# Adj tiles stored in memory as four column pieces

## The chip, the cores and the metric
The kernel runs on one core of a Trainium2 chip. The metric is the time of one execution on the device in microseconds, lower is better; of several runs the median counts.

## The reference
N = 4096 rows, D = 512. `adj` is a sparse 0/1 matrix whose entries get rarer with growing row and column number.
```
q = x @ Wq.T + bq ;  k = key @ Wk.T + bk ;  v = value @ Wv.T + bv
s = (q @ k.T) / sqrt(4096) * adj
s = where(|s| < 1e-5, -1e9, s)
out = layernorm(x + softmax(s) @ v @ Wm.T + bm)
```

## The kernel before
Rows are split into T = 32 row tiles of 128 rows (row r*32 + t is in tile t). In each row tile only few of the 4096 columns have an entry in adj. The kernel finds these columns, gathers the rows of key, of the projected values and of the transposed adj that belong to them (CH = 3 chunks of 128 slots per tile), and does dense attention on 384 slots.

*Reading adj.* The host has laid adj out as `adj_tiles[t]`, 128 x 4096 floats, 16 KB in a row for each partition, 2 MB a tile. SP loads tile t into one of two buffers (`load_adj`, L326 to L329), as soon as the DVE has freed it. The DVE folds each tile with an OR of its two halves (L898), which frees the buffer, and three steps of max and one reduction (L901 to L909) into flags per group of columns. After 8 tiles PE transposes the flags (`lists`), and the DVE picks the slots by six rounds of max and replace (`take_8`, L931, L933) and writes indices.

*First stage.* SP's queue holds, in this order: wv in pieces, the constants, adj tiles 0 to 3, wq and wk, adj tiles 4 to 19, the x tiles 0 to 3, eight copies from `key` into the left half of a `table` in memory (L353, 512 rows of 2 KB each), adj tile 20, a block of xT, adj tile 21. ACT's queue holds wmT and eight blocks of valueT (L715, rows of 8 KB), and between them the value rows that PE and ACT have made, as eight writes into the right half of `table` (L729, 2 KB pieces). PE makes the value rows (L487) and the first q block (L496). GpSimd gathers keys, adj columns and, once the value rows have landed, values for row tiles 0 and 1; for row tile 2 and later it gathers whole table rows (4 KB, L392) and waits for all copies of key before the first (L444).

*Second stage.* PE goes through 32 row tiles: scores, values of the tile before, transposes of the next keys (L578) and adj columns (L593), a q unit (L496), transposes of the weights (L612). In iteration i the DVE takes the score product (`soften`, L1030), the weights (L1045), the sum with x (L1061) and then one more adj tile (`reduce_tile`) of the tiles 20 to 31. SP issues one x tile (waiting for L1061 of the iteration) and behind it the next adj tile, so a tile is loaded during one iteration and used in the next. From row tile 16 on the slots come from these later tiles.

Of the kernel before, what the change touches and what calls it, by code (L numbers as in the profile page):

```python
# [12 lines left out]
P = 128  # L13
N = 4096
D = 512
DC = D // P
T = N // P
# [19 lines left out]
INV_SCALE = 1.0 / float(N) ** 0.5  # L37
MASKED = -1e9
TINY = 1e-5

C_ID = 0
C_DESC = C_ID + P
# [16 lines left out]
def build(nc, adj_tiles, adj_cols, key, valueT, x, xT, wq, wk, wv, wmT, bm, consts, table, out):  # L59
    with ExitStack() as ctx:  # L60
# [3 lines left out]
        def sem(name):  # L64
            return ctx.enter_context(nc.semaphore(name))
# [26 lines left out]
        adj_buf = [big[:, i * 4096:(i + 1) * 4096] for i in range(2)]  # L92
# [66 lines left out]
        adj_in = [sem(f"adj_in{i}") for i in range(2)]  # L159
# [119 lines left out]
        def one_tile(ap, t):  # L279
            return ap[bass.ds(t, 1)].rearrange("a p d -> p (a d)")  # L280

        def wait_apart(eng, s, value):
            eng.wait_ge(s, value)
            eng.sem_inc(passed, 1)

        def trees_of(i):

            t = FIRST + i - (i > LIST_AT[2])
            return [t] if i != LIST_AT[2] and t < T else []
# [13 lines left out]
        def finish_of(i):  # L303

            return sqrt_of(i) if i >= T - 1 else sqrt_of(i - 1)
# [4 lines left out]
        @contextmanager  # L310
        def overflow(eng):
            eng.wait_ge(rounds_ready, 1)
            n = eng.value_load(rounds_i[0:1, 0:1], min_val=0, max_val=MAXR)
            with eng.If(n > 0):
                eng.wait_ge(again, 1)
                yield n
# [3 lines left out]
        @block.sync  # L320
        def _(sp):
            def load_xT(nb):
                sp.wait_ge(q_ps, DC * (nb - 1))
                sp.dma_start(col_buf[nb % 2], xT[nb]).then_inc(cols_in[nb % 2], 16)

            def load_adj(t):  # L326
                if t >= 2:
                    sp.wait_ge(adj_used, t - 1)
                sp.dma_start(adj_buf[t % 2], adj_tiles[t]).then_inc(adj_in[t % 2], 16)  # L329

            def load_x(t):
                if t >= XB:
                    sp.wait_ge(y_sb, t - XB + 1)
                sp.dma_start(x_buf[:, t % XB, :], x_tiles[t]).then_inc(x_in[t % XB], 16)

            def store(t):
                sp.wait_ge(fin_sb, t + 1)
                sp.dma_start(out_tiles[t], y_buf[:, t % YB, :]).then_inc(stored[t % YB], 16)

            for e in range(DC):  # L340
                sp.dma_start(v_left[:, e, :], wv[e * P:(e + 1) * P, :]).then_inc(weights2_in[e], 16)
            sp.dma_start(cst[:, :], consts).then_inc(cst_in, 16)
            sp.dma_start(bm_row, bm).then_inc(bm_in, 16)
            for t in range(4):
                load_adj(t)
            sp.dma_start(w_left, wq.rearrange("(e p) d -> p e d", p=P)).then_inc(weights_in, 16)
            sp.dma_start(w_right, wk.rearrange("(e p) d -> p e d", p=P)).then_inc(weights_in, 16)
            for t in range(4, FIRST):
                load_adj(t)
            for t in range(XB):  # L350
                load_x(t)
            for nb in range(NB):
                sp.dma_start(table[nb * 512:(nb + 1) * 512, 0:D], key[nb * 512:(nb + 1) * 512, :]).then_inc(table_in, 16)  # L353
            for t in trees_of(0):
                load_adj(t)
            for i in range(T + 1):
                for t in finish_of(i - 1):
                    store(t)
                if i % 4 == 0 and i // 4 + 2 < NB:
                    load_xT(i // 4 + 2)  # L360
                if i >= 1 and i + XB - 1 < T:
                    load_x(i + XB - 1)
                for t in trees_of(i + 1):
                    load_adj(t)
            for t in finish_of(T):
                store(t)
            for i in range(YB):
                sp.wait_ge(stored[i], 16 * (T // YB))
            sp.sem_inc(again, 1)

            with overflow(sp) as n:
                with sp.Fori(0, n) as r:
                    with sp.Fori(0, NB) as nb:
                        wait_apart(sp, g_q_sb, (r * NB + nb) * DC + 1)
                        sp.dma_start(g_xT, xT[bass.ds(nb, 1)].rearrange("a p d n -> p (a d) n")).then_inc(g_xT_in, 16)
                sp.wait_ge(g_p_all, 2)
                with sp.Fori(0, T) as t:
                    sp.dma_start(g_x, one_tile(x_tiles, t)).then_inc(g_x_in, 16)
                    wait_apart(sp, g_fin, t + 1)
                    sp.dma_start(one_tile(out_tiles, t), g_y).then_inc(g_stored, 16)  # L380
                    wait_apart(sp, g_stored, t * 16 + 16)
# [495 lines left out]
        def _(dve):  # L877
# [144 lines left out]
            def soften(t):  # L1022
# [9 lines left out]
                dve.wait_ge(abs_sb, t + 1)  # L1032
                nc.vector.tensor_scalar(size[:, :], size[:, :], TINY, MASKED, ALU.is_lt, ALU.mult).then_inc(tiny_sb, 1)
                dve.wait_ge(tiny_sb, t + 1)
# [71 lines left out]
            with overflow(dve) as n:  # L1106
# [7 lines left out]
                with dve.Fori(0, n) as r:  # L1114
# [21 lines left out]
                    with dve.Fori(0, NB) as nb:  # L1136
                        block_no = r * NB + nb
                        for j in range(4):
# [6 lines left out]
                            wait_apart(dve, g_soft, it * 4 + 1)  # L1145
                            nc.vector.tensor_scalar(size[:, :], score[:, 0:SLOTS], TINY, MASKED, ALU.is_lt, ALU.mult
                                                    ).then_inc(g_soft, 1)
                            wait_apart(dve, g_soft, it * 4 + 2)
                            nc.vector.scalar_tensor_tensor(size[:, :], score[:, 0:SLOTS], -TINY, size[:, :],
                                                           ALU.is_gt, ALU.mult).then_inc(g_soft, 1)  # L1150
# [60 lines left out]
def layout(adj, key, value, x, Wq, Wk, Wv, Wm, bq, bk, bv, bm):  # L1211

    import numpy as np

    a = adj.reshape(P, T, K4, P, G8)
    const = np.zeros((P, C_ALL), np.float32)
    p = np.arange(P)
    const[:, C_ID:C_ID + P] = np.eye(P)
    const[:, C_DESC:C_DESC + GK] = GK - np.arange(GK)

    const[:, C_GRP:C_GRP + P] = (p % G8)[:, None] == (p // SPC)[None, :]
    const[:, C_SEL:C_SEL + BT] = (p // G8)[:, None] == np.arange(BT)[None, :]

    const[:, C_BK] = N + p // SPC
    const[:, C_BA:C_BA + T] = (T * (N + p // SPC))[:, None] + np.arange(T)[None, :]
    const[:, C_THR:C_THR + MAXR - 1] = [GS * q for q in range(1, MAXR)]
    const[:, C_NEG] = MASKED
    const[:, C_EPS] = 1e-5
    const[:, C_BV] = 2 * const[:, C_BK] + 1
    const[:, C_TWO] = 2.0 * (p % G8 == G8 - 1)  # L1230
    const[:, C_GRP2:C_GRP2 + P] = const[:, C_GRP:C_GRP + P]
    const[:, C_GRP2 + P - 2:C_GRP2 + P] = 0.0
    for i, b in enumerate((bq, bk, bv)):
        const[:, C_B + i * DC:C_B + (i + 1) * DC] = b.reshape(DC, P).T
    return {
        "adj_tiles": np.ascontiguousarray(a.transpose(1, 3, 0, 2, 4)).reshape(T, P, N),
        "adj_cols": np.concatenate([adj.reshape(P, T, N).transpose(2, 1, 0).reshape(N * T, P),
                                    np.zeros((G8 * T, P), adj.dtype)]),
        "key": key,
        "valueT": np.ascontiguousarray(value.reshape(NB, 512, DC, P).transpose(0, 3, 2, 1)),  # L1240
        "x": x,
        "xT": np.ascontiguousarray(x.reshape(P, NB, T // NB, DC, P).transpose(1, 4, 3, 2, 0)).reshape(NB, P, DC, 512),
        "wq": Wq, "wk": Wk, "wv": Wv, "wmT": np.ascontiguousarray(Wm.T),
        "bm": bm.reshape(1, D),
        "consts": const,
    }
# [19 lines left out]
```

## Time and profile before

| | |
|---|---|
| median of 3 runs | 562.37 us (561.5 to 562.74) |
| the profiled execution | 560.05 us, of it 558.2 us from first to last instruction (span) |
| busy, share of the span | PE 92%, DVE 60%, POOL 42%, ACT 41% |
| mean DMA rate | 288 GB/s, 160.81 MB moved |
| DMA queue q1 (SP) | 20,690 packets, 102.21 MB |
| DMA queue q10 (ACT) | 6,240 packets, 19.92 MB |
| DMA queue q0 (GpSimd) | 16,992 packets, 38.26 MB |
| granted TensorE clock, mean | 0.973 |

The mean shares hide stages: PE is busy nearly throughout, but with different things ahead of it. The tables by stretches of time and the chain of waits have to be read before one can say what a transfer is worth.

### The profile page before, as it was taken

The numbers are of one execution on the slowest core, as the hardware profiler recorded it, in microseconds if no ns is written. First come the engines' busy times: TensorE is split into PE (matmuls) and PEld (weight loads), VectorE is DVE, ScalarE is ACT, GpSimd is POOL, SyncE is SP. The second block draws the span as 40 slices with busy tenths as digits, with TensorE's granted clock in tenths as the row PEclk, the third lists the DMA queues.
The fourth block names the chain that finished last, engine by engine and source line by source line (L and its number), as shares of the span: only waits on it lengthen the run. The fifth ranks groups of instructions, "written<-read, shape, count | busy, mean of one in ns | idle before, by whom it ended". The sixth has DMA issues, their size and how long they took to land.

```text
span 558.2 us, 5679 instructions
## 1 busy us (share of the span) xinstructions
PE 510.8 (92%) x1678; PEld 267.3 (48%) x1678; DVE 337.4 (60%) x756; ACT 229.7 (41%) x463; POOL 232.0 (42%) x205
## 2 busy tenths in 40 slices
PE   6999999999389974999999989999999999999983
PEld 3444444444134443556555545555555555555651
DVE  1574678976961047678688888765645543453552
ACT  0233123333123222334552554464373464465473
POOL 3000020008600366466675565655664565466400
PEclk9999999999879996999999999999999999999996
DMA  9999999999999999595899899656547455346422
GB/s 350 423 406 426 426 422 387 384 397 418 408 395 356 340 418 389 175 360 206 320 383 408 318 292 354 217 162 212 164 150 242 105 182 187 99 144 227 114 76 79
DMA packets 43957, 160.81 MB, mean 288 GB/s; under 512 B 9874, under 2 KB 9874, under 8 KB 37778
## 3 DMA queue, kind: packets, MB, share of 16 engines
q1 hardware_dynamic: 20690, 102.21, 47.0%
q0 software_dynamic: 16992, 38.26, 22.3%
q10 hardware_dynamic: 6240, 19.92, 9.0%
q8 instruction: 15, 0.25, 0.2%
q14 instruction: 20, 0.16, 0.1%
HBM read 161.98 MB, written 25.17 MB: 335 GB/s over the span
## 4 chain that ended last, share of the span: by engine, by line
PE 43%; DMA 22%; DVE 19%; SPq 8%; ACT 4%; issue 3%; POOL 0%; ACTq 0%; DVEq 0%; POOLq 0%
DMA big<-adj_tiles 16%; PE bank L496 13%; PE bank L602 11%; PE bank L622 10%; SPq L353 7%; DVE big L898 7%; PE bank L578 5%; DMA table<-key 4%; DMA kv<-table,index 2%; PE bank L612 1%; DVE big L933 1%; DVE slots L931 1%; PE bank L593 1%; DVE big L901 1%; DVE score L1035 1%
## 5 line engine op out<-in xcount | busy, mean ns | idle before, releaser
L392 POOL DMA_INDIRECT kv<-table,index x90 | 100.1, 1112 | 111.5 <-PE bank L622 89.2
L487 PE MATMUL bank<-kv,big 128*128 128x512 f32 x256 | 113.6, 604 | 10.6 <-DMA big<-valueT 10.6
L496 PE MATMUL bank<-big,M 128*128 128x512 f32 x256 | 120.0, 596 | 0.0
L421 POOL DMA_INDIRECT adj_g<-adj_cols,index x96 | 107.8, 1123 | 29.3 <-issue 29.3
L898 DVE TENSOR_TENSOR big<-big 128x2048 bf16<-128x2048 f32 x32 | 73.2, 2288 | 41.3 <-DMA big<-adj_tiles 41.3
L602 PE MATMUL bank<-keyT,qT 128*128 128x384 f32 x256 | 88.9, 490 | 6.2 <-issue 4.9
L622 PE MATMUL bank<-kv,probT 128*128 128x512 f32 x192 | 89.7, 604 | 0.9 <-ACT probT L809 0.6
L487 PEld LDWEIGHTS bank<-kv,big 128*128 128x128 f32 x256 | 49.1, 193 | 72.6 <-issue 61.0
L602 PEld LDWEIGHTS bank<-keyT,qT 128*128 128x128 f32 x256 | 47.6, 190 | 46.7 <-issue 19.1
L496 PEld LDWEIGHTS bank<-big,M 128*128 128x128 f32 x256 | 44.6, 192 | 34.2 <-issue 34.2
L1030 DVE SCALAR_TENSOR_TENSOR score<-bank,c_cols,adjT 128x384 f32<-128x384 f32 x32 | 19.8, 618 | 67.8 <-PE bank L602 66.4
L578 PEld LDWEIGHTS bank<-cst,kv 128*128 128x128 f32 x384 | 44.9, 144 | 26.4 <-issue 15.5
L578 PE MATMUL bank<-cst,kv 128*128 128x128 f32 x384 | 48.6, 278 | 9.1 <-DMA kv<-table,index 8.3
L622 PEld LDWEIGHTS bank<-kv,probT 128*128 128x128 f32 x192 | 36.7, 193 | 41.0 <-issue 32.6
L783 ACT ACTIVATE keyT<-bank 128x512 f32<-128x512 f32 x96 | 50.2, 592 | 5.1 <-PE bank L578 5.1
L795 ACT ACTIVATE size<-score 128x384 f32<-128x384 f32 x32 | 16.6, 518 | 79.2 <-DVE score L1030 79.2
L772 ACT ACTIVATE qT<-bank,u_col 128x512 f32<-128x512 f32 x32 | 22.0, 687 | 41.5 <-PE bank L496 41.5
L802 ACT ACTIVATE score<-score,new_max 128x384 f32<-128x384 f32 x32 | 19.7, 616 | 40.3 <-DVE new_max L1038 40.3
L428 POOL MEMSET kv<- 128x4096 f32 x1 | 3.5, 3511 | 67.9 <-PE bank L546 67.9
L1045 DVE TENSOR_SCALAR score<-score 128x382 f32<-128x382 f32 x32 | 13.7, 428 | 23.7 <-ACT score L802 23.7
L724 ACT ACTIVATE qT<-bank 128x512 f32<-128x512 f32 x16 | 9.6, 597 | 43.3 <-PE bank L487 43.3
L402 POOL DMA_INDIRECT kv<-key,index x6 | 7.3, 1222 | 48.0 <-DVE index L951 46.5
(99 smaller groups left out, 522.4 us busy)
## 6 DMA issues: line engine op xcount, KB each, us to landing
big<-adj_tiles SPq DMA_DIRECT2D x32, 2048.0 KB, 11.3
big<-valueT ACTq DMA_DIRECT2D x8, 1024.0 KB, 13.4
x_buf<-x SPq DMA_DIRECT2D x32, 256.0 KB, 4.5
table<-key SPq DMA_DIRECT2D x8, 1024.0 KB, 22.8
out<-y_buf SPq DMA_DIRECT2D x32, 256.0 KB, 3.7
big<-xT SPq DMA_DIRECT2D x6, 1024.0 KB, 12.0
table<-qT ACTq DMA_DIRECT2D x4, 1024.0 KB, 20.9
table<-y_buf ACTq DMA_DIRECT2D x4, 1024.0 KB, 28.5
```

What stands on the lines that cost most here:

```text
L353: sp.dma_start(table[nb * 512:(nb + 1) * 512, 0:D], key[nb * 512:(nb + 1) * 512, :]).then_inc(table_in, 16)
L392: pool.indirect_dma_start(kv[:, b, c, :], None, table, bass.IndirectOffsetOnAxis(index[:, t, c:c + 1], 0), bounds_check=N - 1, oob_is_err= ...
L421: pool.indirect_dma_start(adj_g[:, b, c, :], None, adj_cols, bass.IndirectOffsetOnAxis(index[:, t, CH + c:CH + c + 1], 0),).then_inc(adj_g ...
L487: mm = nc.tensor.matmul(bank[4 + t % 2][:, :], col_buf[nb % 2][:, d, k * P:(k + 1) * P], G[:, d, :], start=(d == 0), stop=(d == DC - 1))
L496: mm = nc.tensor.matmul(ps[:, :], M[:, d, a * P:(a + 1) * P], col_buf[nb % 2][:, d, :], start=(d == 0), stop=(d == DC - 1))
L578: mm = nc.tensor.transpose(key_bank[c][:, a * P:(a + 1) * P], kv[:, t % KV, c, a * P:(a + 1) * P], ident)
L602: mm = nc.tensor.matmul(bank[3][:, 0:SLOTS], qT[:, t // 4 % QB, a, t % 4 * P:(t % 4 + 1) * P], keyT[:, a, :], start=(a == 0), stop=(a == D ...
L622: mm = nc.tensor.matmul(bank[5][:, :], probT[:, c * P:(c + 1) * P], kv[:, t % KV, c, D:2 * D], start=(c == 0), stop=(c == CH - 1))
L772: nc.scalar.activation(qT[:, nb % QB, a, :], ps[:, :], ACT.Identity, bias=u_col[:, a:a + 1]).then_inc(q_sb, 1)
L783: nc.scalar.activation(keyT[:, :, c * P:(c + 1) * P], key_bank[c][:, :].rearrange("p (a k) -> p a k", a=DC), ACT.Copy).then_inc(keyT_sb, 1)
L898: nc.vector.tensor_tensor(t1, adj_buf[t % 2][:, 0:2048], adj_buf[t % 2][:, 2048:4096], ALU.logical_or).then_inc(adj_used, 1)
L1030: nc.vector.scalar_tensor_tensor(s, bank[3][:, 0:SLOTS], c_cols[:, t:t + 1], adjT[:, :], ALU.add, ALU.mult).then_inc(prod_sb, 1)
```

## The change
The host lays each adj tile out as four pieces of 1024 columns, each 128 x 1024 floats. A partition's 16 KB are then four runs of 4 KB, 512 KB apart. The load names the buffer as (partition, piece, column) and the source in the same order, so the buffer receives the same bytes at the same places. Nothing else changes: the count of loads, their order and their semaphores stay.
```diff
+PIECES = 4
...
-                sp.dma_start(adj_buf[t % 2], adj_tiles[t]).then_inc(adj_in[t % 2], 16)
+                sp.dma_start(adj_buf[t % 2].rearrange("p (j n) -> p j n", j=PIECES), adj_tiles[t].rearrange("j p n -> p j n")
+                             ).then_inc(adj_in[t % 2], 16)
...
-        "adj_tiles": np.ascontiguousarray(a.transpose(1, 3, 0, 2, 4)).reshape(T, P, N),
+        "adj_tiles": np.ascontiguousarray(
+            a.transpose(1, 3, 0, 2, 4).reshape(T, P, PIECES, N // PIECES).transpose(0, 2, 1, 3)),
```

## Rows read from the trace of the kernel before

**Rows 1.** Windows table: window, length, busy us (instructions) per engine, granted clock, DMA share, GB/s
```profile
0.00:141.00 141.00, 136.67 (x323) 60.29 (x324) 91.54 (x148) 39.34 (x92) 23.26 (x16) 1.00 1.00 404
141.00:201.00 60.00, 46.50 (x133) 22.36 (x132) 25.81 (x59) 15.94 (x34) 15.60 (x16) 0.91 1.03 377
201.00:217.00 16.00, 7.38 (x20) 3.27 (x19) 9.03 (x19) 2.91 (x7) 12.55 (x11) 0.81 0.99 396
217.00:268.00 51.00, 50.18 (x190) 29.34 (x189) 38.09 (x79) 20.09 (x41) 28.96 (x24) 0.96 0.73 267
268.00:336.00 68.00, 62.40 (x234) 34.72 (x233) 54.24 (x122) 34.95 (x67) 43.05 (x37) 1.00 0.95 349
336.00:558.00 222.00, 207.69 (x784) 117.30 (x784) 118.69 (x333) 116.51 (x224) 108.57 (x105) 0.98 0.53 169
```

**Rows 2.** View of one line, L329: its issues, ns min/median/max, first to last start
```profile
L329 SPq DMA_DIRECT2D big<-adj_tiles x32: 327/334/3622, 3.6 to 337.6; - x32
```

**Rows 3.** Chain of waits, 140 to 217 us: start us, us, what
```profile
140.41 0.33 SPq L329
...
180.26 20.32 DMA table<-key
...
204.01 12.64 DMA kv<-table,index
```

**Rows 4.** Timeline of GpSimd: start us, us, instruction, idle before it and releaser
```profile
201.40 1.00 POOL L392 DMA_INDIRECT kv<-table,index  x1 [3.37 <-DMA table<-key]
```

**Rows 5.** Timeline of PE, same columns
```profile
155.14 16.22 PE L487 MATMUL bank<-kv,big 128*128 128x512 f32 x32 [10.60 <-DMA big<-valueT]
...
216.69 2.82 PE L578 MATMUL bank<-cst,kv 128*128 128x128 f32 x12 [8.32 <-DMA kv<-table,index]
...
232.79 0.49 PE L612 MATMUL bank<-cst,score 128*128 128x128 f32 x3
```

**Rows 6.** DMA view, 52 to 58 us; by queue: packets, MB, share of 16 engines
```profile
q1 hardware_dynamic: 144, 2.11, 82.2%
q10 hardware_dynamic: 223, 0.46, 19.5%
```

**Rows 7.** DMA view, 36 to 39.5 us (wq and wk, rows of 2 KB)
```profile
DMA packets 625, 1.42 MB, mean 406 GB/s; under 512 B 29, under 2 KB 29, under 8 KB 611
```

**Rows 8.** DMA view, 206 to 211 us
```profile
q1 hardware_dynamic: 103, 1.32, 62.5%
q0 software_dynamic: 277, 0.69, 36.8%
```

**Rows 9.** DMA view, 160 to 171 us, queue of SP (copies of key, beside q10)
```profile
q1 hardware_dynamic: 1157, 2.30, 60.4%
```

**Rows 10.** DMA view, 186 to 190 us, queue of SP (copies of key, nearly alone)
```profile
q1 hardware_dynamic: 666, 1.32, 102.4%
```

**Rows 11.** Timeline of the DVE: start us, us, instruction, idle before it and releaser
```profile
206.06 2.29 DVE L898 TENSOR_TENSOR big<-big 128x2048 bf16<-128x2048 f32 x1 [5.56 <-DMA big<-adj_tiles]
...
216.81 2.27 DVE L898 TENSOR_TENSOR big<-big 128x2048 bf16<-128x2048 f32 x1
...
227.06 0.62 DVE L1030 SCALAR_TENSOR_TENSOR score<-bank,c_cols,adjT 128x384 f32<-128x384 f32 x1 [5.18 <-PE bank L602]
...
230.20 0.42 DVE L1045 TENSOR_SCALAR score<-score 128x382 f32<-128x382 f32 x1 [0.78 <-ACT score L802]
```

**Rows 12.** Timeline of SP, one issue of an adj tile
```profile
288.29 0.43 SPq L329 DMA_DIRECT2D big<-adj_tiles  x1
```

**Rows 13.** View of L329, its issues from 264 to 326 us, time to landing
```profile
DMA to landing us min/median/max: 9.6/10.7/11.3
```

**Rows 14.** Chain of waits, start of the OR of one tile
```profile
300.79 2.29 DVE big L898
```

**Rows 15.** DMA view, 60 to 141 us, queue of SP
```profile
q1 hardware_dynamic: 1642, 24.02, 73.4%
```

**Rows 16.** Page, DMA issues: what, count, KB each, median us to landing
```profile
big<-valueT ACTq DMA_DIRECT2D x8, 1024.0 KB, 13.4
```

## The prediction

> **What bounds the kernel now.** I read the windows table first, because this kernel has stages with different limits [rows 1]. Its column "DMA share" is the busy share of the 16 DMA engines. Up to 217 us it stands at 0.99 to 1.03: the transfers never rest. From 217 to 268 it is 0.73 while PE is busy for 50.2 of 51 us, from 268 to 336 DVE shares the chain with PE, and after 336 us PE is busy for 208 of 222 us with DMA at 0.53. The last adj tile is issued at 337.6 us [rows 2]. So the change can only act at three places: the saturated stretch, its end, and the stretch from 268 to 336.
>
> The chain of waits says what ends the saturated stretch. The DVE works through adj tiles 0 to 19, mostly waiting for the next tile. When it frees a buffer at 140.41 us SP issues tile 19, then four x loads and eight copies of key into the table; the last copy is issued at 180.26 and lands 20.32 us later, at T = 200.6 [rows 3]. GpSimd has waited 3.37 us for exactly that [rows 4], issues the three gathers of row tile 2, the last at 204.01, and PE, which idled for 8.3 us, starts on them at 216.69 [rows 3, 5]. From there on PE leads. So two numbers matter: when T comes, and how long the gather takes after T (16.05 us).
>
> **The change, part by part.** The same 2 MB per tile arrive, at the same places of the buffer, and no DVE, PE or ACT instruction changes. Each partition's 16 KB now come as four runs of 4 KB that lie 512 KB apart. A DMA engine moves 8 partitions of a tile, so it gets 32 packets of 4 KB where it had 8 of 16 KB. Three things follow, and a fourth at the end.
>
> *1. More packets on saturated engines.* Between 52 and 58 us both sizes run side by side [rows 6]. q1: 2.11 MB are 129 packets of 16 KB; 82.2% of 16 x 6 us are 78.9 us, 612 ns each. q10: 0.46 MB are about 223 packets of 2 KB; 18.7 us, 84 ns each. With time = fixed + bytes x rate this gives 0.0368 ns per byte and 8.6 ns fixed per packet. Then 24 more packets per tile and engine cost 0.21 us, 4.1 us for the 20 tiles before T. A second reading is by rates: 2.57 MB in 6 us are 428 GB/s in that window, 406 where 2 KB rows of the weights run almost alone [rows 7]. A tile of 2.10 MB is 4.90 or 5.17 us; 0.27 us over 56 more packets is 4.8 ns each, so 24 of them are 0.12 us, 2.3 us for 20 tiles. Ends: 2.3 us and, if 4 KB were as dear as 2 KB, 5.4 us. I take 3.2 us, between the two readings. Nothing hides it: the share is 1.00 before 141 us and 1.03 after.
>
> The Trainium skill (DMA: Bandwidth & Descriptors, "iDMA fabric — 4 AXI ports for 8 engines, asymmetric across TPBs") has 408.7 GB/s for a stream of loads with 4 KiB rows; at that rate a tile would take 5.13 us, 0.23 us more than at 428 GB/s, and 20 tiles 4.6 us, 1.4 us more than I take. No row here has such loads on SP's queue.
>
> *2. A different split between the queues.* Where two queues have work, the packets alternate. From 206 to 211 us q1 moves 1.32 MB in xT and adj packets, about 100, and q0 moves 0.69 MB, about 170 packets of at most 4 KB; q1 takes 62.5% of the time and q0 36.8% [rows 8]. One for one, with a few engines already out of q1 work, gives that. With 4 KB packets adj gets a smaller share beside ACT's queue (valueT, value rows of the table) and those land sooner. PE's one stall of the first stage, 10.6 us for valueT at 155.14 us [rows 5], should nearly go. It is off the chain: PE waits for the gather anyhow, so this only makes its later idle longer. T itself needs all of that traffic done, in whatever order, and the engines were full before, so the order alone does not move T. One side effect does. The key copies then run more by themselves. From 160 to 171 us beside q10 a 2 KB packet of theirs took 60.4% of 176 us over 1123 packets, 95 ns [rows 9]; alone, from 186 to 190 us, 102.4% of 64 us over 645, 102 ns [rows 10]. There are 256 per engine: 0 if nothing shifts, 1.8 us if all did. I take 1.2 us.
>
> *3. The gather after T.* On the engine that reaches T last, q1 still holds tile 20 (8 packets), an xT block (8 of about 306 ns, half of 612) and tile 21 (8): 12.3 us. The gather of row tile 2 has 24 packets per engine; by size one is 8.6 + 4096 x 0.0368 = 159 ns. I let its first packets come at T + 2.8: it is issued at T + 0.8, and with 2 us from there the count meets the trace, as follows. Alternating from there, q1's remaining 19.4 packets (9.5 us) pair with 19.4 gather packets (3.1 us), and 4.6 gather packets follow (0.7 us): T + 16.1. The trace has T + 16.05. With 4 KB packets q1 has 17.6 of tile 20's 32 done by T + 2.8; then 24 pairs, 14.4 with adj (0.318 us), 8 with xT (0.465 us), 1.6 with adj: 8.8 us. The gather ends at T + 11.6, 4.4 us sooner.
>
> Some of it is lost on the DVE, which now gets its tiles later. Tile 20 landed at T + 5.4 (DVE starts at 206.06 after 5.56 us of waiting [rows 11]); alternating it lands at about T + 7.4. Tile 21 was there before the DVE asked for it at 216.81; now, paired with the gathers of row tile 3, it lands at about T + 20. The DVE can then start the score product of row tile 2 at T + 25.3 (5.1 us after that OR, as 227.06 - 5.18 - 216.81 [rows 11]), where PE would offer it at T + 22.0 (227.06 less 4.4). These 3.3 us meet 2.0 us of slack: the weights are ready at about 230.8 and PE transposes them at 232.79 [rows 5, 11]. So 1.3 us are given back and 3.1 us kept. Ends: 0 (the DVE eats it all, or packets do not alternate) and 4.4.
>
> The Trainium skill (same page, "Queues, rings and completion order") says that a DMA engine drains a whole packet of typically 9 to 17 descriptors of one ring before it switches. Taken literally the split would go by groups of about the same bytes for q0 and this part would give 0 instead of 3.1 us. The counts of [rows 8] do not tell groups of 8 from single ones; the two readings part only after the change.
>
> *4. The stretch from 268 to 336 us.* SP issues a tile once per iteration. The one issued at 288.29 landed 11.3 us later, at 299.6, and the DVE began on it at 300.79 [rows 12, 13, 14]: 1.2 us of slack. The tiles issued from 264 to 326 us took 9.6 to 11.3 us. A tile gets 0.12 to 0.21 us longer by packets and somewhat more from the adj_g gathers that run beside it. SP's own instruction is a DMA issue of 0.43 us and may grow; the copies of key show that the queue takes 512 rows per DMA. Below the slack this costs 0; at 1 us too late per tile it would be 6 us. I take 0.3 us.
>
> **Sum.** +3.2 + 1.2 - 3.1 + 0.3 = +1.6 us. The profiled execution had 558.2 us of span in 560.05 us; the median of the runs is 562.37. So 559.8 in span and 564.0 as a time.
>
> **Rivals.**
> *Stalls of the 16 KB packets go (faster).* From 60 to 141 us q1's 1466 data packets took 73.4% of 1296 us, 649 ns each instead of 612 [rows 15]. Something slows reads for a while. If it is how 16 engines walk through 16 KB rows in step, a layout with other distances ends it: 37 ns x 8 packets x 11.5 tiles is 3.4 us, which turns 564.0 into 560.6. It decides from 1.6 us of relief on. For it: the slow packets were in a stretch with adj nearly alone. Against: the same share could be paid by any layout, and the new one could also add such stalls (the same 3.4 us upward, 567.4). Chance 0.24.
> *No alternation gain (slower).* The gather still lands at T + 16, because an engine serves the queues in larger groups or the DVE's late tiles hold everything: 564.0 + 3.1 = 567.1. Chance 0.17.
> *Late tiles (slower).* From 268 to 336 us tiles land over 1.2 us later than now, and the DVE waits in each of some six iterations. At 2 us late beyond the slack over three to six tiles: +6 to +12, about 571. Decides from 12.5 us issue to landing. Chance 0.08.
> *Nothing (same).* Costs and gain cancel or the packets are priced by bytes: 562.4. Chance 0.13.
> *Forecast*, 562.9 to 565.5: chance 0.38.
>
> **Numbers.** A measurement of this kernel tells changes of about 0.2%, 1.1 us. The forecast is just above that bound, so of its 0.38 some 0.11 are within it. Faster by over 0.2%: 0.24 plus a little of the others, 0.26. Within: 0.13 + 0.11 + 0.02 = 0.26. Slower: 0.48. The range holds the stall relief on one side and the missing gather gain with 4 KB as dear as 2 KB on the other: 559.5 to 568.5; late tiles and a larger relief stay outside.
>
> **What would show it.** q1 has some 12,300 packets more. Landing of valueT and of the value rows well below before (valueT 13.4 us, median [rows 16]), PE's stall at 155 us gone. T at 203 to 206 us. From T to PE's restart 11 to 14 us instead of 16. DVE waiting for tile 20 and tile 21. Tiles after 268 us landing in 10 to 12.5 us with no DVE wait. The prediction is wrong if T moves by less than 2 or more than 6 us, or if PE restarts as long after T as now.

## The result, and the profile after

The changed kernel takes 571.59 us (median of 4 runs, 569.89 to 571.98), the kernel before 561.93 us (4 runs in the same comparison): ratio 1.0175, 95% interval 1.0133 to 1.0217. I had forecast 564.0 us within 559.5 to 568.5. It is slower, as forecast, but by 9.7 us instead of 1.6, and outside the range. The profiled execution took 571.98 us with 570.1 us of span. It lies 11.9 us above the profiled one of the kernel before, while the medians lie 9.7 us apart, so what the traces show below is a little larger than the typical difference.

The queues in the changed kernel, from its page (queue: packets, MB, share of 16 engines), show that the packets changed as expected: 12,288 more on q1, the same bytes.
```profile
q1 hardware_dynamic: 32978, 102.21, 47.6%
q10 hardware_dynamic: 6240, 19.92, 8.9%
```
The windows table of the changed kernel (columns as in [rows 1]):
```profile
60.00:90.00 30.00, 30.00 (x73) 13.27 (x71) 19.94 (x22) 7.49 (x19) 3.51 (x1) 1.00 0.95 356
90.00:115.00 25.00, 18.07 (x45) 7.77 (x44) 16.39 (x34) 7.35 (x18) 0.00 (x0) 0.92 1.02 403
115.00:125.00 10.00, 4.73 (x11) 2.95 (x12) 9.66 (x19) 0.00 (x0) 0.00 (x0) 0.53 0.31 105
125.00:165.00 40.00, 40.00 (x97) 17.63 (x97) 19.14 (x30) 13.61 (x33) 21.06 (x18) 1.00 1.01 400
```
and two of the same windows in the kernel before:
```profile
60.00:90.00 30.00, 30.00 (x73) 13.35 (x72) 20.30 (x25) 8.00 (x20) 3.51 (x1) 1.00 1.02 415
115.00:125.00 10.00, 10.00 (x25) 4.42 (x24) 6.26 (x16) 3.73 (x9) 1.07 (x1) 1.00 1.01 398
```
There is a hole: from 115 to 125 us the DMA engines are busy for 0.31 of the time where they were full, 6.9 us of transfer time lost, and PE is busy for half of the window. Already from 60 to 90 us the engines move 356 GB/s instead of 415. No window of [rows 1] before 217 us has such a hole.

The waits that make the hole, from PE's timeline of the changed kernel (start us, us, instruction, idle before it and releaser):
```profile
120.27 1.42 PE L518 MATMUL bank<-cst,big 64*128 64x8 f32 x6 [12.20 <-DVE big L941]
...
188.35 5.84 PE L562 MATMUL bank<-kv,keyT 128*128 128x512 f32 x8 [16.49 <-DVE keyT L1019]
...
228.93 1.63 PE L580 MATMUL bank<-cst,kv 128*128 128x128 f32 x12 [2.90 <-DMA kv<-table,index]
```
and from the DVE's, first of the kernel before, then of the changed one:
```profile
90.10 2.29 DVE L898 TENSOR_TENSOR big<-big 128x2048 bf16<-128x2048 f32 x1 [0.46 <-DMA big<-adj_tiles]
```
```profile
103.92 2.29 DVE L900 TENSOR_TENSOR big<-big 128x2048 bf16<-128x2048 f32 x1 [2.92 <-DMA big<-adj_tiles]
```
This is the OR of tile 11, the last before the DVE makes the first list. It comes 13.8 us later. PE reaches unit 17, behind which it spreads that list's slots (L516 before, L518 now), at 108 us as ever, but the list is ready only at 120 us. In the kernel before the list was ready at 106.7 us (end of L939), 1.9 us before PE came to L516 at 108.64. The stall at 155.14 us for valueT [rows 5] is gone, as predicted; these two came instead. While PE waits it makes no value rows, so ACT's queue has nothing to load or store. The DVE works on the list and frees no adj buffer, so SP's queue has nothing to load either. Both queues run dry together. In the kernel before the DVE made the same list, SP's queue ran dry just the same, and ACT's queue filled the engines alone (DMA view, 105 to 110 us, then the changed kernel, 115 to 125 us):
```profile
q10 hardware_dynamic: 660, 2.03, 100.4%
q1 hardware_dynamic: 1, 0.00, 0.0%
```
```profile
q1 hardware_dynamic: 257, 0.99, 29.0%
q10 hardware_dynamic: 42, 0.07, 1.8%
```

The key copies then land late. GpSimd's first gather from the table, changed kernel (answers to [rows 4]), and the chain around it (answers to [rows 3]):
```profile
215.00 1.00 POOL L394 DMA_INDIRECT kv<-table,index  x1 [8.60 <-DMA table<-key]
```
```profile
195.10 19.09 DMA table<-key
217.60 11.28 DMA kv<-table,index
```
T is 214.2 instead of 200.6, 13.6 us later. The gather ends 14.7 us after it instead of 16.05. PE restarts at 228.93 instead of 216.69, 12.2 us later, and the span is 11.9 us longer. The whole loss is made before T. The other stall, 16.49 us for L1019, is not on the way to T: the key copies on SP's queue do not wait for it, and in e9 below it is longer (22.32 us) while T comes 7.1 us sooner.

### The profile page after: what moved, and what is told of

The parts are those of the page before. It is cut to its first block, busy times and chain, and to the rows that moved or that the text cites. A ratio compares the mean times of both kernels' runs of the same rounds, so it can differ in the third digit from the quotient of the medians.

```text
span 570.1 us, 5679 instructions
## 1 busy us (share of the span) xinstructions
PE 511.6 (90%) x1678; PEld 267.2 (47%) x1678; DVE 336.4 (59%) x756; ACT 229.5 (40%) x463; POOL 231.0 (41%) x205
## 4 chain that ended last, share of the span: by engine, by line
PE 45%; DMA 26%; DVE 16%; SPq 5%; issue 4%; ACT 3%; POOL 0%; ACTq 0%; DVEq 0%; POOLq 0%
DMA big<-adj_tiles 21%; PE bank L498 14%; PE bank L604 11%; PE bank L624 11%; DVE big L900 6%; PE bank L580 5%; SPq L355 5%; DMA table<-key 3%; DMA kv<-table,index 2%; PE bank L614 1%; PE bank L595 1%; DVE big L935 1%; DVE slots L933 1%; DVE big L903 1%; DVE score L1037 1%
## 5 line engine op out<-in xcount | busy, mean ns | idle before, releaser
L394 POOL DMA_INDIRECT kv<-table,index x90 | 96.5, 1072 | 114.9 <-PE bank L624 86.9
L423 POOL DMA_INDIRECT adj_g<-adj_cols,index x96 | 111.6, 1162 | 29.3 <-issue 29.3
L580 PE MATMUL bank<-cst,kv 128*128 128x128 f32 x384 | 47.4, 273 | 3.7 <-DMA kv<-table,index 2.9
L774 ACT ACTIVATE qT<-bank,u_col 128x512 f32<-128x512 f32 x32 | 22.0, 687 | 41.4 <-PE bank L498 31.4
## 6 DMA issues: line engine op xcount, KB each, us to landing
table<-qT ACTq DMA_DIRECT2D x4, 1024.0 KB, 15.6
table<-y_buf ACTq DMA_DIRECT2D x4, 1024.0 KB, 16.8
```

Source lines behind the costliest of these rows:

```text
L394: pool.indirect_dma_start(kv[:, b, c, :], None, table, bass.IndirectOffsetOnAxis(index[:, t, c:c + 1], 0), bounds_check=N - 1, oob_is_err= ...
L423: pool.indirect_dma_start(adj_g[:, b, c, :], None, adj_cols, bass.IndirectOffsetOnAxis(index[:, t, CH + c:CH + c + 1], 0),).then_inc(adj_g ...
L580: mm = nc.tensor.transpose(key_bank[c][:, a * P:(a + 1) * P], kv[:, t % KV, c, a * P:(a + 1) * P], ident)
L774: nc.scalar.activation(qT[:, nb % QB, a, :], ps[:, :], ACT.Identity, bias=u_col[:, a:a + 1]).then_inc(q_sb, 1)
```

## Experiments

Theory S: packets of 4 KB lose turns against ACT's queue and cost a fixed time each; the adj tiles come late, the list comes late, and both queues run dry. Theory D: reading pieces that lie 512 KB apart is slow. Each ratio is to runs of the kernel before on the same chip as the variant. Traces are of one execution each, and their T varies: with 16 KB runs in the first stage it is 200.6 (before), 201.3 (e3) and 206.8 us (e10), with four pieces 214.2 (changed), 215.9 (e4) and 217.3 us (e1).

**e1: the four runs side by side.**
```diff
-        "adj_tiles": ... .reshape(T, P, PIECES, N // PIECES).transpose(0, 2, 1, 3)),
+        "adj_tiles": np.pad(a.transpose(1, 3, 0, 2, 4).reshape(T, P, PIECES, N // PIECES),
+                            ((0, 0), (0, 0), (0, 0), (0, 64))),
...
-                sp.dma_start(..., adj_tiles[t].rearrange("j p n -> p j n")
+                sp.dma_start(..., adj_tiles[t][:, :, 0:N // PIECES]
```


> The four 4 KB runs of a partition lie side by side in memory (256 B of padding between them keeps them apart), so packets stay 4 KB and the distance of 512 KB is gone. Theory S (the size of the packets costs turns beside ACT's queue and a fixed time each): as the changed kernel, 570 to 573 us, PE waits some 12 us for the DVE near 120 us, the DMA engines have a hole there. Theory D (reading pieces 512 KB apart is slow): as the kernel before, 561 to 564 us, and 4 KB packets of adj take about 159 ns on average instead of 171.

Measured: 572.52 us, ratio 1.0199 (1.0137 to 1.0261). The hole is the same:
```profile
115.00:125.00 10.00, 4.45 (x10) 2.87 (x11) 9.66 (x19) 0.00 (x0) 0.00 (x0) 0.50 0.39 136
```
Theory D falls: the distance between the pieces costs nothing that shows in the kernel's time. It is the length of the run.

**e2: two pieces of 8 KB.**
```diff
-PIECES = 4
+PIECES = 2
```


> Two pieces of 8 KB per partition, 1 MB apart. S: the share beside valueT (8 KB) is even instead of one third, beside the value rows (2 KB) 4 to 1 instead of 2 to 1, and a third of the fixed costs: about 564 to 567 us, the wait for the list near 115 us shorter or gone. D: pieces far apart as well, so near the changed kernel's 571 us.

Measured: 565.26 us, ratio 1.0057 (0.9987 to 1.0127). In the profiled execution, the fastest of the four at 561.39 us, PE's wait for the list is 3.2 us. The time lies in between, as S says; the interval alone does not exclude no change.

**e3 and e10: 4 KB only behind T.** Tiles 0 to 19 in 16 KB runs, tiles 20 to 31 in pieces.
```diff
-                sp.dma_start(adj_buf[t % 2], adj_tiles[t]).then_inc(adj_in[t % 2], 16)
+                if t >= FIRST:
+                    sp.dma_start(adj_buf[t % 2].rearrange("p (j n) -> p j n", j=PIECES),
+                                 adj_pieces[t - FIRST].rearrange("j p n -> p j n")).then_inc(adj_in[t % 2], 16)
+                else:
+                    sp.dma_start(adj_buf[t % 2], adj_tiles[t]).then_inc(adj_in[t % 2], 16)
...
-        "adj_tiles": np.ascontiguousarray(a.transpose(1, 3, 0, 2, 4)).reshape(T, P, N),
+        "adj_tiles": np.ascontiguousarray(tiles[:20]),
+        "adj_pieces": np.ascontiguousarray(tiles[20:].reshape(-1, P, PIECES, N // PIECES).transpose(0, 2, 1, 3)),
```


> Tiles 0 to 19 in runs of 16 KB as before, tiles 20 to 31 in four pieces of 4 KB. Only the stretch after the key copies can change. My part 3 (gather of row tile 2 sooner, 3.1 us kept): 558 to 560 us, with the last key copy landing at about 200.6 as before and PE restarting 12 us after it instead of 16. Rival (the DVE's late tiles take it all back): 561 to 563 us. S and D both leave the first stage as it was.

> The kernel with 16 KB runs for tiles 0 to 19 and 4 KB pieces for tiles 20 to 31 again, with more rounds. Its gather of row tile 2 ended 14.0 us after the last key copy instead of 16.1, and nothing else moved: 1 to 3 us faster than the kernel before, ratio 0.994 to 0.999. If the first look was chance: ratio 1.000 +- 0.002.

Measured: 559.97 us, ratio 0.996 (0.9899 to 1.002), and with more rounds 558.65 us (12 runs), ratio 0.996 (0.9931 to 0.9989). So the second half of the change by itself is a gain of 0.4%. The chain of e3:
```profile
181.45 19.86 DMA table<-key
204.73 10.55 DMA kv<-table,index
215.32 2.82 PE bank L583 x12
```
T is 201.3, the gather ends at 215.3, 14.0 us later (before: 16.05). That is 2.0 us of the 4.4 I had worked out; I had expected 12 us.

The profiled execution of e10 (561.7 us, the second slowest of its 12 runs) shows something that the expectation did not foresee. Its first stage is that of the kernel before, with 16 KB runs, and yet tile 11 is folded at 96.42 us instead of 90.10, PE waits for the list, and T is 206.8:
```profile
112.77 1.42 PE L521 MATMUL bank<-cst,big 64*128 64x8 f32 x6 [4.54 <-DVE big L944]
```
So the 1.9 us of slack ahead of this wait do not hold in every execution, even without pieces. From T to PE's restart it takes 13.8 us there, as in e3.

**e4: 4 KB only before T**, the reverse of e3.

> Tiles 0 to 19 in four pieces, tiles 20 to 31 in runs of 16 KB. If all the loss is in the first stage: T at about 214 us as in the changed kernel and then 16 us to PE's restart instead of 14.7, so 571 to 574 us. If the loss sits partly behind 268 us: 567 to 570 us.

Measured: 572.8 us, ratio 1.0191 (1.013 to 1.0252). T is 215.9 us and PE restarts at 231.28, 15.4 us later. All of the loss that shows is in the first stage.

**e5: PE asks later for the list.**
```diff
-                if t == 17:
+                if t == 21:
                     pe.wait_ge(prep_sb, 2 * DC)
                     spread_slots(0)
```


> The changed kernel, but PE spreads the slots of the first list (L518) four value units later, after unit 21 instead of 17, so it no longer stands still at 108 us for the DVE's list. Theory S, part hole (with adj late and PE waiting, both queues have nothing to load near 115 to 125 us, some 7 us lost): the DMA share there rises above 0.8 and the time falls by 4 to 7 us, to 565 to 568 us. Rival (the hole only shifts, or the loss is all in slower and more packets): 570 to 572 us.

Measured: 567.25 us, ratio 1.0105 (1.0023 to 1.0188). The hole is mostly filled, with tile 11 still folded at 103.3 us:
```profile
115.00:125.00 10.00, 10.00 (x28) 4.65 (x27) 9.69 (x18) 3.67 (x9) 0.00 (x0) 1.00 0.87 259
```
PE now waits 7.8 us for the flags of the second eight tiles (L506) and 14.4 us for L1019, both made by a DVE that is still late.

**e6: the same edit on the kernel before.**

> The same edit on the kernel before, as a control. There the DVE's list was ready before PE asked, so nothing waits and the time stays at 560 to 563 us. A gain here too would say that the edit helps for another reason.

Measured: 561.24 us, ratio 0.9995 (0.9961 to 1.0028). Without the late list the edit does nothing that shows.

**e7: valueT in runs of 2 KB, adj in 4 KB.**
```diff
-                act.dma_start(col_buf[j % 2], valueT[j] if j < NB else xT[j - NB]).then_inc(cols_in[j % 2], 16)
+                act.dma_start(col_buf[j % 2], valueT[j].rearrange("d p n -> p d n") if j < NB else xT[j - NB]
+                              ).then_inc(cols_in[j % 2], 16)
...
-        "valueT": np.ascontiguousarray(value.reshape(NB, 512, DC, P).transpose(0, 3, 2, 1)),
+        "valueT": np.ascontiguousarray(value.reshape(NB, 512, DC, P).transpose(0, 2, 3, 1)),
```


> The changed kernel with valueT laid out so that its loads have runs of 2 KB instead of 8 KB. Per turn ACT's queue then moves 2 KB beside 4 KB of adj, so adj has two thirds of the time beside both kinds of ACT transfers, where beside valueT it has one third now. If lost turns cause the loss: tile 11 is folded earlier than 103.9 us, PE's wait for the list shrinks from 12.2 us, 566 to 569 us. If only the number of packets counts: 1.6 us slower than the changed kernel by 192 more packets per engine at 8.6 ns, 572 to 574 us.

Measured: 565.7 us, ratio 1.0105 (1.0065 to 1.0146). This is just below the 566 to 569 expected. The loads of valueT have 4,096 packets where they had 1,024, and the kernel's median got faster. Tile 11 is folded at 97.03 us instead of 103.92, and PE waits 4.7 us for the list instead of 12.2:
```profile
97.03 2.29 DVE L901 TENSOR_TENSOR big<-big 128x2048 bf16<-128x2048 f32 x1 [2.50 <-DMA big<-adj_tiles]
```
```profile
113.39 1.42 PE L518 MATMUL bank<-cst,big 64*128 64x8 f32 x6 [4.70 <-DVE big L942]
```
How the two queues share the engines is seen from 45 to 50 us, with 4 KB packets of adj beside 2 KB packets of ACT's queue:
```profile
q1 hardware_dynamic: 338, 1.32, 66.9%
q10 hardware_dynamic: 336, 0.69, 36.0%
```
They move equal numbers of packets, and so the one with twice the size moves twice the bytes. Cutting the rival's packets gives adj its turns back. How much that is worth varies: e9 has the same transfers up to tile 11 and folds it at 100.06 us.

**e9: both edits.**

> The changed kernel with both edits, the later spreading of the first list and valueT in runs of 2 KB. Theory S says that what is left is what no order of turns gives back: 20 tiles x 0.23 us for more packets (bench, 5.12 against 4.89 us per tile) and 8 valueT blocks x 24 packets x 9.5 ns = 1.8 us, less about 2 us of the sooner gather: 4.4 us above the kernel before, 564 to 566 us, and no stretch before the last key copy with a DMA share below 0.9. If the two edits mend the same hole, it is no faster than the better of the two, 565.7 us; if their gains add up, 561 to 562 us.

Measured: 564.55 us (12 runs), ratio 1.0049 (1.0029 to 1.007), an interval wholly below the changed kernel's. T is near 207.1 and the two windows show no hole:
```profile
60.00:90.00 30.00, 30.00 (x74) 13.25 (x73) 20.23 (x25) 7.49 (x19) 3.51 (x1) 1.00 1.02 391
115.00:125.00 10.00, 10.00 (x27) 4.75 (x28) 9.69 (x16) 3.32 (x9) 0.00 (x0) 1.00 0.99 341
```
What is left, 3.6 us, is of the size of the 4.4 us expected for the packets' own cost less the sooner gather.

**e8: the transfers by themselves.** It leaves out all of the reference's work: seven phases of ten tile loads, each tile folded once by the DVE, in a single execution.
```
for t in range(10): wait until buffer t % depth is folded; load tile t
phase: 1 whole, 2 buffers | 2 pieces, 2 | 3 near, 2 | 4 whole, 4 | 5 pieces, 4
       6 whole, 2, beside ACT's loads and stores | 7 pieces, 2, beside them
```


> Not the reference's work: seven phases of ten adj tile loads of 2 MB each, the DVE folds each tile once, the output is zeros. Phases: 1) 16 KB runs, two buffers; 2) four pieces 512 KB apart, two buffers; 3) four pieces side by side, two buffers; 4) as 1 and 5) as 2 with four buffers; 6) as 1 and 7) as 2 with ACT's queue loading valueT (8 KB) and storing 2 KB pieces. By packet times of 612 and 159 ns: 1) 49 to 52 us, 2) and 3) 51 to 54 us, 4) and 5) 49 and 51 us. If 4 KB loads cannot keep the engines full with two tiles in flight: 2) and 3) over 55 us at a DMA share below 0.95, and 5) well below them. Alternation by single packets: in 7) ACT's transfers land in about half the time they need in 6).

The windows table, from the OR of the first tile of a phase to that of the tenth (columns: window, length, DVE, POOL, clock, DMA share, GB/s), phases 1 to 5, and then the parts of phases 6 and 7 in which ACT's queue has work:
```profile
8.50:62.10 53.60, 20.64 (x9) 0.00 (x0) 1.00 0.90 343
72.69:127.82 55.13, 20.63 (x10) 0.00 (x0) 1.00 0.90 333
139.08:191.28 52.20, 20.63 (x9) 0.00 (x0) 1.00 0.93 348
201.90:245.94 44.04, 20.64 (x10) 0.00 (x0) 1.00 0.96 411
256.32:302.79 46.47, 20.63 (x9) 0.00 (x0) 1.00 0.99 398
315.42:350.00 34.58, 12.28 (x6) 0.00 (x0) 1.00 1.01 418
390.57:426.00 35.43, 9.17 (x5) 0.00 (x0) 1.00 1.03 420
```
Three things are read from it.

*Packets.* With four buffers a tile takes 4.89 us in 16 KB runs (44.04 / 9) and, between two ORs in the middle of phase 5, 5.12 us in pieces: 0.23 us more, 9.5 ns for each of 24 packets.

*Two buffers.* With nothing beside them a tile takes 5.96, 6.13 and 5.80 us in phases 1 to 3, and the engines are full for 0.90 to 0.93 of the time, in either layout. Pieces that lie apart took 0.33 us more than pieces side by side; with ORs 5.0 to 8.2 us apart within a phase, one execution does not tell whether that is the distance. Two buffers need not leave such gaps, though. In the last 20 us of phase 7 ACT's queue is done, there are still two buffers, and pieces follow each other every 5.11 to 5.14 us on full engines (DMA view, 431 to 451 us):
```profile
q1 hardware_dynamic: 2036, 8.09, 101.0%
```
What decides between the two states was not found.

*Beside ACT's queue.* A tile takes 6.6 us in 16 KB runs (315.42 to 375.18, nine tiles) and 8.9 us in pieces (390.57 to 426.00, four tiles), while ACT's stores land in 31.3 us (median) in phase 6 and 22.3 in phase 7:
```profile
DMA to landing us min/median/max: 25.7/31.3/43.8
```
```profile
DMA to landing us min/median/max: 14.1/22.3/24.5
```
From the first issue to the tenth OR, however, phase 6 takes 70.0 us (305.19 to 375.18) and phase 7 74.0 us (377.66 to 451.64). The tiles lose turns early and catch up when ACT's queue is done. Of the 4.0 us more, 2.3 are the packets of ten tiles; where no work waits across the two streams, the order of the transfers costs at most the other 1.7.

The expectation that phases 1 to 3 separate the layouts was wrong, and ACT's transfers in phase 7 were expected in half the time of phase 6; they took 0.7 of it.

## Why the prediction was wrong

**Part 1, the price of a packet: right in kind, too small.** I took 3.2 us for 20 tiles, between two readings of 2.3 and 4.1. Phases 4 and 5 of e8 give 20 x 0.23 = 4.6 us. The sentence of the Trainium skill (DMA: Bandwidth & Descriptors, "iDMA fabric — 4 AXI ports for 8 engines, asymmetric across TPBs"), 408.7 GB/s for 4 KiB rows, gave an estimate of 4.6 us too, and phase 5 agrees: 2.097 MB in 5.12 us are 410 GB/s. The lower reading came from comparing rates in two windows with different company; the difference of single packet times (8.6 ns) was the better one.

**Part 2, the order of the transfers: this is the step that failed.** I wrote that "the engines were full before, so the order alone does not move T", and so put this term at nothing. The time up to T in the two traces shows what it was (windows table, kernel before, then changed):
```profile
0.00:200.60 200.60, 182.77 (x452) 82.25 (x453) 117.35 (x206) 54.88 (x125) 38.86 (x31) 0.97 1.01 396
0.00:214.20 214.20, 180.12 (x430) 80.65 (x431) 113.69 (x198) 52.83 (x120) 37.81 (x31) 0.93 0.97 370
```
By the queues' shares in these windows (100.9% and 96.9% together) the transfers took 202.4 and 207.6 us. Of the 13.6 us by which T moved, 5.2 are more transfer time, near the 4.6 for packets, and 8.4 are time in which the engines were not full. Nearly all of these are in two places, the hole (6.9 us) and the stretch from 60 to 90 us (a share of 0.95 instead of 1.02, 2.1 us); the other stretches take back 0.6. The 1.2 us that I took for the key copies are inside the 5.2, and no run separates them.

The step took a share of 1.00 as a property of the engines that any order of the transfers would keep. It nearly holds in e8 (1.7 us at most beyond the packets), where the streams do not wait for each other. In the kernel they do: the DVE needs the tiles to make the list, PE needs the list to go on, and ACT's queue needs PE. Before the change the DVE's list was 1.9 us ahead of PE, and while the DVE finished it and SP's queue was empty, ACT's queue had enough work left to fill the engines (100.4% from 105 to 110 us). With 4 KB packets ACT's transfers land sooner (its stores from y_buf in 16.8 us instead of 28.5, median), the tiles lose turns while they do (8.9 us each instead of 6.6 in e8), and tile 11 is folded 13.8 us later, of which the packets themselves explain 12 x 0.23 = 2.8 us. The list becomes late, PE's wait stops ACT's queue as well, and the engines idle. I had seen PE's units and the DVE's tiles as two streams that only share the engines, and never named the wait at L516 that joins them.

The stretch from 60 to 90 us is not explained by this. A backlog of ACT's queue is not what kept the engines full there before: from 80 to 90 us it moved almost nothing in either kernel (DMA view, kernel before, then changed).
```profile
q1 hardware_dynamic: 268, 3.87, 101.4%
q10 hardware_dynamic: 10, 0.02, 0.4%
```
```profile
q1 hardware_dynamic: 799, 3.20, 87.4%
```
Nor is it that 4 KB packets cannot fill them: in e7 they do (100.0% from 80 to 90 us), and in the last 20 us of phase 7. The share from 60 to 90 us also differs between executions with the same layout, 0.93 (e1), 0.95 (changed kernel) and 0.99 (e4) with pieces, 0.97 in e10 without. It looks like the two states that two buffers show in e8, and its cause stays open.

That the hole and the turns are causes, and not company, is shown by three edits. e5 takes PE's wait away and leaves tile 11 as late as before: the share in the hole goes from 0.31 to 0.87, the ratio from 1.0175 to 1.0105. e7 gives the turns back: tile 11 comes 6.9 us sooner (3.9 in e9), 1.0105. e9 does both: 1.0049. e6 is the control, and e1 rules out the distance. The intervals of e5 and e7 overlap the changed kernel's, that of e9 does not, so what each of the two is worth by itself is known only roughly.

**Part 3, the gather: right in mechanism, half in size.** I kept 3.1 us of 4.4. Measured from T it ends 1.4 us sooner in the changed kernel, 2.0 in e3. From the first gather of row tile 2 to PE's restart the seven traces with pieces behind T (changed kernel, e1, e3, e5, e7, e9, e10) take 12.7 to 14.0 us, mean 13.4, and the three with 16 KB runs (before, e4, e6) 14.6 to 17.0, mean 15.6: 2.3 us. The queues alternate by packets, as I had it. The DMA view of the changed kernel from 219.2 to 221 us:
```profile
q1 hardware_dynamic: 78, 0.41, 55.7%
q0 software_dynamic: 81, 0.33, 45.9%
```
78 packets beside 81. What was off is the start. I let the gather's packets flow from T + 2.8; in the changed kernel, from T = 214.2 to 219.2, and in e4, where tile 20 has 16 KB packets, from T = 215.9 to 220.4:
```profile
q1 hardware_dynamic: 447, 2.11, 102.2%
q0 software_dynamic: 2, 0.01, 0.4%
```
```profile
q1 hardware_dynamic: 159, 1.95, 102.1%
```
They come only at about T + 5, with either size of packet, by when q1 has moved 2 MB undisturbed. My sum with this start (31.4 packets of 4 KB done, then 24 pairs in 8.8 us) gives T + 13.8, 2.3 us sooner than T + 16.1, which is what the traces have. For 16 KB packets the sum stays at T + 16.1. Tile 20 was not late either: the DVE began on it at T + 5.1 (0.6 us of waiting), where I had T + 7.4, and on tile 21 at T + 17.7 (1.8 us of waiting), where I had T + 20. Why the first packets need over 4 us from their issue at 215.00 was not found. The Trainium skill (DMA: Bandwidth & Descriptors, "Queues, rings and completion order") has a rule of typically 9 to 17 descriptors of one ring before a switch. I had read it as turns of about the same bytes, which would have cost the gain. That reading does not hold here: the shares follow the number of packets. Whether a turn is one packet or an equal group on both sides the counts do not tell.

**Part 4, behind 268 us: nothing.** The DVE waits for no adj tile there in the changed kernel, and the way from PE's restart to the end is 341.2 us instead of 341.5.

**The rivals and the signs.** Relief from stalls did not come. "No alternation gain" and "late tiles" named a slower result, but for other causes. The late tiles were those of the first stage, where I had looked only at bytes. Of the signs of being wrong, T moving by more than 6 us came true. That the result is slower, as I forecast, is mostly luck: my +1.6 us was the balance of small terms, and the largest of the real ones was not among them.

## What to carry to other kernels

A DMA share of 1.00 does not say that the transfers are the only bound: ask which queue fills the engines while the other has nothing to load, and what becomes of that when it is served sooner. The length of a run is also a weight in the split between queues, because two busy queues here moved equal numbers of packets; long runs belong to the stream that others wait for, short ones to the stream that may wait. Before changing that split, list the waits between the two streams' consumers with the slack each has now; here it was 1.9 us, and in one execution (e10) it was used up even without pieces. The same edit costs 1.9% in the first stage (e4) and gives 0.4% behind it (e10), so it should be made for tiles 20 to 31 only.

## What the runs showed of the hardware

Two loads of 2 MB in flight, each buffer freed 2.3 us after landing, filled the 16 engines to 0.90 to 0.93 in three phases of e8 and fully (101.0%) in the last 20 us of a fourth; four in flight gave 0.96 to 0.99. Two queues with work moved equal numbers of packets, 338 of 4 KB beside 336 of 2 KB in 5 us (e7). Cutting valueT's packets from 8 to 2 KB, with more packets on full engines, made the kernel's median faster (e7; the intervals just overlap). A gather issued from GpSimd moved 2 packets in the 4.2 us after its issue beside 4 KB packets of SP's queue, and none in the 3.7 us after its issue beside 16 KB packets (e4).
